# Softmax denominators from a ones column, transposed blocks grouped over four heads, q copy on VectorE, null value at the projection

## The reference, cut to what matters

```python
# 16 heads of 64, one key/value head for all of them, plus one "null" key and value
q = layernorm(x) @ Wq                      # (b, 16, n, 64)
k, v = split(... @ Wkv)                    # (b, n, 64) each
sim = concat([q @ null_k + null_bias, q @ k.T + bias], axis=-1)
sim = where(causal and mask, sim, -big)    # causal: query i sees keys 0..i
attn = softmax(sim)                        # over n + 1 columns
out = attn @ concat([null_v, v])           # (b, 16, n, 64)
x = x + layernorm(out.reshape(b, n, 1024) @ Wout) * g_out
```

## Time and profile before

| | us |
|---|---|
| median of 3 runs | 1735.9 (1734.8 to 1736.44) |
| the profiled execution, its own time | 1732.54 |
| its span, from the first to the last instruction | 1730.6 |
| before the first `biased` of the loop | 89.6 |
| the sixteen stages of attention, to the last `biased` | 1264.8 |
| the rest: the last unit, and the two layers of experts | 376.2 |

### The profile page before, as it was taken

How to read it: one execution, slowest core, us unless ns; L and a number is a source line. 1 busy time by engine, 2 the same in 40 slices (tenths; PEclk the granted TensorE clock), 3 DMA queues, 4 the chain that set the end, 5 groups by cost and what they waited for, 6 DMA issues and landing times.

```text
span 1730.6 us, 46424 instructions
## 1 busy us (share of the span) xinstructions
PE 1470.3 (85%) x16377; PEld 1081.0 (62%) x16377; DVE 1410.4 (81%) x3651; ACT 1210.2 (70%) x3064; POOL 751.0 (43%) x1412
## 2 busy tenths in 40 slices
PE   2467778888889999977888888999999799999998
PEld 1245556666677777766666666777777555555555
DVE  4557778888889999977788888999999687777777
ACT  1268778888889899978888888989999432332232
POOL 5557776443434334366554232223222365522222
PEclk9779999999999999989999999999999899999999
DMA  4002122111211223012121212221223000000000
GB/s 138 7 24 62 51 62 75 57 62 69 75 58 67 87 99 99 33 44 62 51 81 52 85 63 75 75 81 62 82 99 99 1 25 19 1 1 1 13 13 25
DMA packets 50440, 96.70 MB, mean 56 GB/s; under 512 B 3332, under 2 KB 27028, under 8 KB 50212
## 3 DMA queue, kind: packets, MB, share of 16 engines
q1 hardware_dynamic: 45504, 90.27, 15.8%
q10 hardware_dynamic: 4708, 3.45, 0.7%
HBM read 91.54 MB, written 2.17 MB: 54 GB/s over the span
## 4 chain that ended last, share of the span: by engine, by line
PE 42%; DVE 21%; ACT 14%; issue 11%; POOL 3%; DMA 1%; DVEq 0%; ACTq 0%; SPq 0%; POOLq 0%
PE tp L1312 7%; DVE p_lo L964 7%; ACT p_hi L722 6%; DVE biased L880 5%; PE sc L1203 3%; PE sc L1086 3%; PE sc L1087 3%; PE sc L1088 3%; ACT q_b L651 3%; PE sc L1204 3%; ACT probs L630 3%; PE op L1086 2%; PE aux L1086 2%; PE tp L1086 2%; PE aux L1088 2%
## 5 line engine op out<-in xcount | busy, mean ns | idle before, releaser
L964 DVE TENSOR_TENSOR p_lo<-tp,p_hi 128x512 f16<-128x512 f32 (+3 forms) x768 | 416.6, 554 | 121.3 <-ACT p_hi L722 114.3
L880 DVE CUSTOM_DVE_ANT_0 biased<-sc,bias,neg_null 128x256 f32<-128x256 f32 (+7 forms) x512 | 411.0, 803 | 2.7 <-issue 0.8
L630 ACT ACTIVATE probs<-biased,neg_max 128x256 f32<-128x256 f32 (+7 forms) x512 | 395.7, 773 | 14.2 <-DVE neg_max L880 12.7
L1312 PE MATMUL tp<-ident,probs 128*128 128x128 f32 x2304 | 388.7, 278 | 17.7 <-DVE p_lo L964 15.5
L722 ACT ACTIVATE p_hi<-tp 128x512 f16<-128x512 f32 (+3 forms) x768 | 368.9, 491 | 43.6 <-PE tp L1312 33.5
L1086 PE MATMUL op<-v_s,p_hi 128*128 128x64 f16 x2304 | 284.9, 194 | 54.4 <-DVE p_lo L964 35.9
L1203 PE MATMUL sc<-k_a,q_a 128*128 128x512 f16 (+3 forms) x768 | 254.2, 331 | 66.2 <-DVE neg_max L880 59.3
L1312 PEld LDWEIGHTS tp<-ident,probs 128*128 128x128 f32 x2304 | 267.9, 142 | 52.9 <-issue 37.9
L1088 PE MATMUL op<-v_s,p_lo 128*128 128x64 f16 x2304 | 284.0, 194 | 0.0
L1087 PE MATMUL op<-v_s,p_hi 128*128 128x64 f16 x2304 | 283.9, 194 | 0.0
L1086 PEld LDWEIGHTS op<-v_s,p_hi 128*128 128x128 f16 x2304 | 216.0, 99 | 85.5 <-DVE p_lo L964 62.1
(11 more groups left out here) (257 smaller groups left out, 3611.4 us busy)
## 6 DMA issues: line engine op xcount, KB each, us to landing
bias<-rel_table SPq DMA_DIRECT2D x4, 2048.0 KB, 8.5
bias<-in_fside_16xSxS SPq DMA_DIRECT2D x4, 2048.0 KB, 7.9
bias<-rel_table SPq DMA_DIRECT2D x4, 1792.0 KB, 7.9
bias<-in_fside_16xSxS SPq DMA_DIRECT2D x4, 1792.0 KB, 7.1
bias<-rel_table SPq DMA_DIRECT2D x4, 1536.0 KB, 7.3
bias<-in_fside_16xSxS SPq DMA_DIRECT2D x4, 1536.0 KB, 6.7
bias<-rel_table SPq DMA_DIRECT2D x4, 1280.0 KB, 5.6
bias<-in_fside_16xSxS SPq DMA_DIRECT2D x4, 1280.0 KB, 6.3
```

Source lines behind the costliest of these rows:

```text
L630: ac.activation(probs[:, i % 2, 0:w], biased[:, i % 2, 0:w], ACT.Exp, bias=neg_max[:, u % 2, i % HU:i % HU + 1], scale=-1.0, accum_out=row ...
L880: ve.tensor_tensor_reduce(out=biased[:, i % 2, 0:w], in0=sc[i % 2][:, 0:w], in1=bias[:, g % 2, i % HU, 0:w], scale=-1.0, scalar=neg_null[: ...
L964: ve.tensor_tensor(p_lo[:, gi % 4, 0:nb * P], tp[gi % 2][:, 0:nb * P], p_hi[:, gi % 4, 0:nb * P], ALU.subtract).then_inc(s["p_lo"], 1)
L1312: last = te.transpose(tp[gi % 2][:, jj * P:(jj + 1) * P], probs[:, n % 2, (j0 + jj) * P:(j0 + jj + 1) * P], ident[:, :])
```

## The change

1. **Denominators.** The values `v_s` get a 65th column, 1 in the upper half and 0 in the lower one. The products of `pv` are 65 columns wide, and the last column of each head in `op` is the sum of its probabilities. The exp on ACT (L630) no longer has a second result. DVE adds `p_null` to the four sums (`denom`), waits for that, takes the reciprocal, waits for that, and then multiplies `op` by it into `o_n`, directly from PSUM. `o_raw` and POOL's `o_n` are gone; the next unit's first `pv` waits for `o_n`.
2. **Groups.** Four blocks make a group whatever head they belong to, within a unit. A unit has 4 nk blocks and so exactly nk groups, all full: 576 in all. A group is split in the step in which its last block is transposed, and multiplied in the step after it.
3. **q copy.** The copy from `q_b` to `q_a` goes from ACT to DVE, ahead of DVE's two lower halves.
4. **Null value.** POOL's `o_null` and `denom` are gone. POOL multiplies `p_null` by the reciprocal into `pn` (128 x 4). For the last group of heads of each tile and sequence (32 times), PE transposes the 16 columns of `pn`, ACT copies them to `pn_t`, and one float32 product of 256 columns with `nv_w` joins the output projection. `nv_w`, the null value times the output weights, is made once a layer by 24 products of 256 columns and a copy on ACT.
5. **Small things.** POOL forms the exponent of `p_null` at k = 2, after the last `biased` rather than the last `probs`. The null value is loaded as a column, and made into a block pattern in two halves before the loop by five short DVE instructions; POOL writes the constants with five more memsets. Three small weight tiles lie inside the second bias buffer, so the second bias load waits until PE has read them.

```diff
 class Plan:
-            for j in range(0, nk, 4):
-                self.groups.append((n, j, min(4, nk - j)))
+            blocks = [(u * HU + h, j) for h in range(HU) for j in range(nk)]
+            for b0 in range(0, len(blocks), 4):
+                group = blocks[b0:b0 + 4]
...
+                self.finished[group[-1][0]].append(len(self.groups))
+                self.group_end.append(events)
+                self.groups.append(group)
...
-        v_s = [sb(f"v_s{i}", [P, B * TILES, 2, DH], F16) for i in range(2)]
+        v_s = [sb(f"v_s{i}", [P, B * TILES, 2, DH + 1], F16) for i in range(2)]
...
 SP:
             load_bias(sp, 0)
+            sp.wait_ge(setup["mt"], 1)
             load_bias(sp, 1)
...
 POOL:
-                if k == 1 and 1 <= m <= NU:
+                if k == 2 and 1 <= m <= NU:
-                    pool.wait_ge(s["o_raw"], u + 1)
                     pool.wait_ge(s["r_den"], u + 1)
-                    gp.tensor_tensor(o_n[:, :, :], o_raw[:, :, :],
-                                     r_den[:, :].unsqueeze(2).to_broadcast([P, HU, DH]), ALU.mult)\
-                        .then_inc(s["o_n"], 1)
+                    gp.tensor_tensor(pn[:, T % 2, bt, hg * HU:(hg + 1) * HU], p_null[:, u % 2, :], r_den[:, :], ALU.mult)\
+                        .then_inc(s["pn"], 1)
...
-                if k == 3 and 0 <= m < NU:
+                if k == 2 and 0 <= m < NU:
-                    pool.wait_ge(s["probs"], HU * (u + 1))
+                    pool.wait_ge(s["biased"], HU * (u + 1))
...
-                    gp.tensor_tensor(denom[:, :], rows[:, u % 2, :], p_null[:, :], ALU.add).then_inc(s["denom"], 1)
...
-                    gp.tensor_tensor(o_null[:, :, :], null_v[:, :].unsqueeze(1).to_broadcast([P, HU, DH]),
-                                     p_null[:, :].unsqueeze(2).to_broadcast([P, HU, DH]), ALU.mult)\
-                        .then_inc(s["o_null"], 1)
...
 ACT:
                     ac.activation(probs[:, i % 2, 0:w], biased[:, i % 2, 0:w], ACT.Exp,
-                                  bias=neg_max[:, u % 2, i % HU:i % HU + 1], scale=-1.0,
-                                  accum_out=rows[:, u % 2, i % HU:i % HU + 1]).then_inc(s["probs"], 1)
+                                  bias=neg_max[:, u % 2, i % HU:i % HU + 1], scale=-1.0).then_inc(s["probs"], 1)
...
-                    act.wait_ge(s["q_hi"], 2 * (u + 1))
-                    ac.activation(q_a[0:DH, u % 2, :], q_b[0:DH, u % 2, :], ACT.Copy).then_inc(s["q_dup"], 1)
...
+                        ac.activation(pn_t[:, u % B, :], turned(pn_ps) if u < U0 else pn_ps, ACT.Copy)\
+                            .then_inc(s["pn_s"], 1)
...
-                        ac.activation(p_hi[:, gi % 4, 0:nb * P], tp[gi % 2][:, 0:nb * P], ACT.Copy)\
-                            .then_inc(s["p_hi"], 1)
+                        ac.activation(p_hi[:, gi % 4, :], tp[gi % 2][:, :], ACT.Copy).then_inc(s["p_hi"], 1)
...
 DVE:
-                    ve.tensor_tensor(o_raw[:, :, :], op[:, 0:UW].rearrange("p (h d) -> p h d", h=HU),
-                                     o_null[:, :, :], ALU.add).then_inc(s["o_raw"], 1)
-                    dve.wait_ge(s["denom"], u + 1)
+                    link(ve.tensor_tensor(denom[:, :], o_ps[:, :, DH], p_null[:, u % 2, :], ALU.add))
+                    if u >= 1:
+                        dve.wait_ge(s["pn"], u)
                     ve.reciprocal(r_den[:, :], denom[:, :]).then_inc(s["r_den"], 1)
+                    dve.wait_ge(s["r_den"], u + 1)
+                    if u >= 1:
+                        dve.wait_ge(s["ot"], u)
+                    ve.tensor_tensor(o_n[:, :, :], o_ps[:, :, 0:DH],
+                                     r_den[:, :].unsqueeze(2).to_broadcast([P, HU, DH]), ALU.mult).then_inc(s["o_n"], 1)
...
                     dve.wait_ge(s["q_hi"], 2 * (u + 1))
+                    ve.tensor_copy(q_a[0:DH, u % 2, :], q_b[0:DH, u % 2, :]).then_inc(s["q_dup"], 1)
...
 PE:
-                if gi == plan.first_group[n] and h == 0 and u >= 1:
-                    pe.wait_ge(s["o_raw"], u)
+                if n % HU == 0 and j == 0:
+                    if u >= 1:
+                        pe.wait_ge(s["o_n"], u)
...
+                for at_, (n, j) in enumerate(plan.groups[gi]):
...
+                    last = three(op[:, h * (DH + 1):(h + 1) * (DH + 1)], p_hi[:, gi % 4, cols], p_lo[:, gi % 4, cols],
+                                 v_hi, v_lo, j == 0, j == nk - 1)
...
+                    if hg == HG - 1:
+                        pe.wait_ge(s["pn_s"], u // UNITS * B + u % B + 1)
+                        last = te.matmul(first[:, 0:D], pn_t[:, u % B, :], nv_w[:, :], start=False, stop=True)
```

More of the change, by code:

```diff
@@ L78, in unit @@
         return n // HU
-    def of(self, n):
-        return range(self.first_group[n], self.first_group[n + 1])
     def at(self, n):
-        return list(self.of(n)) if 0 <= n < self.steps else []
+        return self.finished[n] if 0 <= n < self.steps else []
     def groups_done(self, n):
-        return self.first_group[n + 1]
+        return max((gi for i in range(n // HU * HU, n + 1) for gi in self.finished[i]), default=-1) + 1
 def model(nc, a, out):
@@ L257, in model @@
                     x_st x_rs xn xt xt_hi xt_lo xr_hi xr_lo kv kv_act kv_r kv_d kv_v k_dup kt k_hi k_lo
-                    d_null p_null denom r_den o_null o_raw o_n ot ot_hi ot_lo y y_s y_acc
+                    d_null p_null r_den pn pn_t pn_s nv_w nv_o o_n ot ot_hi ot_lo y y_s y_acc
                     y_st y_rs y_n x_new""")
@@ L422, in _ @@
             gp.memset(ones64[:, :], 1.0).then_inc(setup["ones"], 1)
+            gp.memset(nv_f, 0.0).then_inc(setup["nv0"], 1)
+            for i in range(2):
+                for hl in range(2):
+                    gp.memset(v_s[i][:, :, hl, DH:DH + 1], 1.0 - hl).then_inc(setup["v1"], 1)
             for e in range(E):
@@ new lines, in small @@
+                    if n in NULL_AT:
+                        layer = NULL_AT.index(n)
+                        take(True, (s["nv_o"], layer + 1))
+                        pe.wait_ge(setup["nvs"], 1)
+                        pe.wait_ge(job_done, job_end[3 * layer + 2])
+                        for c in range(INNER // P):
+                            last = three(second[0:H, 0:D], nv_s[:, 0, c, :], nv_s[:, 1, c, :],
+                                         wo[layer][:, 0, c, :], wo[layer][:, 1, c, :], c == 0, c == INNER // P - 1)
+                        last.then_inc(s["nv_w"], 1)
```

167 lines of the change are left out of this document (103 added, 64 removed).

## The result

The changed kernel took **1835.5 us** (median of four runs, 1834.7 to 1844.5), the kernel before 1736.2 beside it: a ratio of 1.058, 95% interval 1.055 to 1.062. The prediction was 1731, with a range up to 1768. It was forecast 5 us faster and is 99 us slower; the forecast missed by 104.

The account below looks back on a forecast made before the run. Attention's time was taken as DVE's work plus its idle time, 1083.1 and 181.7 us. Work +56, idle -70 and rest +9 gave -5 against the profiled 1732.5, so 1727.5, with the median at 1731; range 1694 to 1768.

Parts of the forecast that it names:

- DVE's work: DVE's work in attention: +41 for denominators, +26 for the q copy, -11 for full groups, +56 us in all.
- Full groups: Splits on DVE: fewer, full-width splits for units with remainders take 11 us off DVE's work.
- The q copy: Copy of q moved from ACT to DVE: 0.20 us each, 26 us of DVE, bounds 13 to 78.
- The denominators: Sum, reciprocal and o_n on DVE: 0.32 us a unit, 41 us of DVE, bounds 10 to 54.
- rival E: DVE's denominator chain: a chained small step costs no more than a free one, 31 us less, 1700; chance 0.05.
- The groups: 35 us come back: DVE's idle time outside full stages: fewer groups mean fewer waits for ACT's p_hi; 24 + 11 = 35 us return.
- A lighter ACT: 35 us: DVE's waits before the splits: ACT relieved, p_hi comes earlier; 35 us less idle, between 0 and 79.
- Small additions: nine: nv_w 5 us, small float32 products and transposes with the 65th column 3, DVE steps before the loop 0.8: together 9.
- B: At k = 1 and k = 3: DVE is the bound, groups give back 35, a lighter ACT nothing; 1766, chance 0.23.
- C: Outside full stages: ACT and POOL had set the pace, DVE's idle share falls to stage 15's 5%; 1682, chance 0.13.
- D: q copy on DVE: it goes at the split's 0.61, 52 us more, 1783; chance 0.05.
- Rival F: q copy on DVE: it is waited out to its end, 17 us more less the small step's, 1743; chance 0.09.

Follow-up runs that it names:

- experiment 6: Changed kernel with groups ending with their head and no null value at the projection: 1749.4 us; with the q copy back on ACT too: 1735.9 us.
- by_head_no_null: Changed kernel with groups that end with their head and without the null value's product at the projection: 1749.4 us (1.0078).
- ones_in_raw: Kernel before plus the ones column alone, denominators from the addition of the null value's share; q copy on ACT, groups ending with their head: 1733.1 us (0.9982).
- q_on_act: Changed kernel with the copy of q's upper half back on ACT: 1829.2 us (1.054).
- the best kernel: Kernel before plus ones column, full groups across heads only at five blocks a head (stages 4, 12): 1727.9 us; with the q copy on DVE 1735.6.
- by_head: Changed kernel with groups that end with their head, as before the change (768 groups): 1801.7 us (1.039).
- no_null: Changed kernel without the null value at the projection (no transposes or copies of pn, no nv_w or its products): 1775.8 us (1.024).
- pn_early: Changed kernel with the transposes of pn beside those of the outputs and POOL's pn earlier, at k = 1: 1794.2 us (1.034).

## Why the prediction was wrong, step by step

**DVE's work** was right in its sum, in part by luck: +58 measured, +56 forecast. Full groups saved 10 (11 forecast). The q copy added 29 to 40 in three pairs of kernels (26 forecast, inside the bounds of 13 to 78). The denominators added 28 of busy time (41 forecast, experiment 6); about 9 more are gaps of 0.03 and 0.04 us in front of the two dependent steps, which count as idle. Too much here and too little at the copy cancelled. The chained small steps hold up the next by 0.18 and 0.22 us in the changed kernel (0.19 and 0.21 forecast):

```profile
606.39 0.15 DVE L888 TENSOR_TENSOR denom<-op,p_null 128x4 f32<-128x4 f32 x1
606.57 0.18 DVE L891 RECIPROCAL r_den<-denom 128x4 f32<-128x4 f32 x1
606.79 0.42 DVE L895 TENSOR_TENSOR o_n<-op,r_den 128x256 f32<-128x256 f32 x1
607.13 1.14 DVE L914 CUSTOM_DVE_ANT_0 biased<-sc,bias,neg_null 128x896 f32<-128x896 f32 x1
```

So rival E, by the sentence of the Trainium skill ("VectorE: DVE Perf Modes", "The DRAIN you can't avoid") that a semaphore costs nothing extra, which the page measures on eight chained copies, doesn't hold for steps of four elements. Yet the chain together with what it takes from ACT and POOL cost the kernel no time (experiment 6): DVE's idle time fell by as much as its work grew. What the chain costs without that relief was not tried.

**"The groups: 35 us come back"** failed in sign: idle time rose by 60 us alone on the kernel before. The step looked at one wait of DVE alone and took its number of waits as the measure of all waiting. Where nk is 1 to 3 that wait did shrink, and DVE stood instead for PE's small work, held up behind products that wait for the longer splits; where nk is 5 to 7 fewer waits were longer in sum. Groups across heads leave steps with nothing and steps with double.

**"A lighter ACT: 35 us"** stays open. Without groups and null value idle time fell by 49 us (181.7 to 132.8 in by_head_no_null) while DVE's work grew by 64; how much of that is ACT's relief and how much is added work that fills waits, no run separates. The relief itself was priced at twice its size, since the prediction priced DVE by what holds up the next instruction but ACT by what its instructions last. A second result of ACT lasts 0.20 us, yet what follows starts 0.09 after it, in the kernel before:

```profile
703.51 0.20 ACT L630 ACTIVATION_READ_ACCUMULATOR probs<-biased,neg_max 128x1 f32 x1
703.60 0.59 ACT L722 ACTIVATE p_hi<-tp 128x512 f16<-128x512 f32 x1
```

512 of them are some 46 us, not 100; ones_in_raw without them has ACT busy for 38 us less. The q copy took 66 us of ACT's busy time (q_on_act beside the changed kernel), not 81.

**"Small additions: nine"** failed by 44 to 52 us. The products and transposes were priced by how long they last (12 us of PE "mostly beside DVE"). Not priced were what `take` waits for before the transpose, a bank whose release stands behind `biased`, the copy and the lower halves on DVE; that POOL's `pn` stands at k = 2 behind its steps on the output's norm; and that scores and transposes of the probabilities stand behind both in PE's queue. The prediction named the queues behind the q copy and the chain, but not that behind the smallest instruction of the change.

**TensorE's clock** had no term, though the earlier trace rows show 0.81 in stage 0. By the estimate in the last section it is about 16 of the 100 us.

**The rivals.** B came nearest in mechanism: it put the place at k = 1 and k = 3 and PE at a `tp` bank or at `o_n`, but let groups give 35 us back and ended at 1766. PE's waits grew at `op` and q's bank far more than at `tp` (14.9 to 18.2), and that for `o_n` is under that for `o_raw` before. Its condition, less than 65 us of idle time back, held: none came back. C's opposite condition failed (DVE's idle share of attention rose from 14 to 16%), and so did D's: the copy's median is 0.285 us, not 0.6. Rival F's mechanism, the copy waited out to its end, held: in stage 6 a copy lasts 0.77 us and the lower halves start 0.80 after its start (last section), and in all 128 units they start 0.03 us after its end. That agrees with the Trainium skill, same page, section "Two Vector instructions with no wait between them", by which an instruction whose output starts in another quarter of the partitions starts only when the earlier ones have finished.

Of the signs named in advance the splits (576 of 0.69), DVE's busy time near 1140, the copy near 0.28 us (by its median) and stage 15 longer came true. Stage 0 shorter and the idle time before the splits did not; 107 us there was the sign named for B. Stages 6, 7, 14 and 15 are 8 to 11 us longer, not 2 to 4.

## What to carry to other kernels

A new instruction in an in-order queue costs what it waits for, not what it lasts: before pricing it, write down which bank or buffer it takes, who frees that, what stands ahead of the freeing step on its engine, and what stands behind the new one. Where three engines hand each other blocks through two banks, merging hand-overs saves work and can still lose time; count per step how many groups finish and how many banks are open. Compare an experiment stage by stage: a move that brought 5 us in all had won 24 in one half of the stages and lost 20 in the other, by a wait that it had made itself. And price every engine by the same measure, what holds up its next instruction.

## What the runs showed of the hardware

The copy of 64x512 float16 elements inside SBUF lasts between 250 and 771 ns on DVE, and what it lasts follows what POOL does. All 128 of the changed kernel:

```profile
L941 DVE COPY q_a<-q_b x128: 250/285/771, 84.0 to 1435.2; 64x512 f16<-64x512 f16 x128
```

62 of them overlap no POOL instruction and last 279 to 288 ns. The 14 that overlap mostly POOL's L531 last 250 to 257. The twelve that overlap mostly POOL's 256-element float32 addition to `x` (L563) last 627 to 771. One of these on DVE, in stage 6, and one that ends beside a small POOL step (L531) in stage 10:

```profile
601.74 0.77 DVE L941 COPY q_a<-q_b 64x512 f16<-64x512 f16 x1
602.54 0.88 DVE L943 TENSOR_TENSOR q_a<-aux,q_b 64x256 f16<-64x256 f32 x2
...
1026.81 0.25 DVE L941 COPY q_a<-q_b 64x512 f16<-64x512 f16 x1
```

In the best kernel with this copy on DVE the same showed: 84 without overlap at 252 to 288 ns, those beside POOL's large float32 steps up to 752. Which path the two engines share was not tried here. The excess over 285 ns is 128 x (0.351 - 0.285) = 8 us in all, DVE work that the prediction had no term for, though its bounds of 13 to 78 us hold it.

The granted clock of TensorE fell with the waiting. Over the whole profiled execution its mean is 0.972 before and 0.959 in the changed kernel. Of the two levels, 1.2 and 2.4 GHz, the lower one was thus granted for 97 and 150 us (the span x 2 x (1 - clock)). It lies mostly in the short stages, where PE stands idle most: stage 0 of the changed kernel has 0.80, with PE busy for 40.3 of 62.5 us. What it costs shows between executions of one kernel. The four of by_head took 1796.3, 1799.5, 1803.8 and 1806.5 us at 0.969, 0.964, 0.963 and 0.959: 10 us for 37 us more at the lower level. Those of q_on_act went from 1820.7 at 0.968 to 1834.7 at 0.956: 14 for 45. As an estimate from these, 0.3 us each, the 53 us more in the changed kernel are worth 16 of its 100 us, and the higher clocks of no_null (0.967 on average) and pn_early (0.969) some 10 of the 60 and 12 of the 41 us that they brought. No run holds the clock fixed, so which part is cause and which effect of the waiting is not shown.
